# TensorE transposes of the unit matrix ahead of the first norm's, and VectorE's small edge operations moved behind the first weight split

## The chip, the cores and the metric

One Trainium2 chip, one core of it. The metric is the device time of one execution in microseconds (us); the kernel before took 716.55 us (median of 3 runs, 715.22 to 717.28).

## What is computed

A graph layer on 384 nodes of width 1024, in float32. The input is normalised, goes through two attention branches side by side, and then through a routed feed-forward attention:

```python
xn = _layernorm(x, axis=-1)
x = x + gnn(xn, edge_index, edge_type, ...) + mix(xn, ...)      # both: 16 heads of 64, 384 x 384 scores
x = x + ffn(_layernorm(x, axis=-1), ...)                        # three hard-routed trees, then attention
```

Only the beginning concerns this change. `mix` makes q, k, v by `x @ Wqkv`; from k it also makes a row of weights, `softmax(sigmoid(relu(k @ W1 + b1) @ W2 + b2))`. `gnn` adds a mask to its scores, which is built from the edge list: `mask[src, dst] = softplus(w)[type - 1]`, the last edge of a pair counting. For the mask the kernel needs softplus of four weights, and for each edge the key `src * 384 + dst`, compared with the keys of the others, so that an earlier duplicate is dropped.

## The kernel before, in words

The weights come as a stream of units, each 1024 x 256 (1 MB), numbered in the order of use: unit 0 (`U_K0`) is the first K of `mix`, unit 1 (`U_A0`) the first of the other branch's projections, unit 2 (`U_Q0`) the first Q. SyncE loads a unit into one of two `raw` slots (L437 for units 0 and 1, L462 for the rest; unit n is loaded once the low part of unit n - 2 has been made). Every product is done in three passes with rounded operands: each float32 value is split into a high part (`w_hi`, `act_hi`) and the rest (`w_lo`, `act_lo`), and hi x hi, lo x hi and hi x lo are added up in PSUM. The high part of a unit is made by ScalarE (`split_hi`, L777; for unit 0 by GpSimd, L503), the low part by VectorE (`split_lo`, L1264) or, for ten units, unit 1 among them, by GpSimd (L476).

The order on each engine is written out by hand, and semaphores tie the engines together. At the start:

- VectorE takes the statistics of the three tiles of 128 rows (`norm`, L1325), and ScalarE scales each tile into `nat` (L841).
- TensorE waits for `consts_ready` (the unit matrix `ident`, made by GpSimd, L480), and `norm_T` (L1952) transposes tile t in eight pieces of 128 x 128, four to a bank, as soon as `nat` of tile t is there. ScalarE copies each bank into `act_hi` (`take_norm`, L829), VectorE subtracts to get `act_lo` (`take_norm`, L1346).
- Between the `take_norm`s of tiles 0, 1 and 2 VectorE has five small operations (L1461 to L1465): half a bias, |w| of the four edge weights (L1462, its two tensor inputs are the same four columns of `pp`, in SBUF), the edge columns cast to float, and the keys (L1465, two SBUF inputs too). ScalarE's Exp at L925 waits for L1462 by `soft_v`; GpSimd reads the results behind its split of unit 1.
- After them comes `split_lo` of unit 0 (L1468), then the copy of the triangle into PSUM (L1471), and then `key_tile(0)` to `key_tile(12)`, 51 comparisons of the edges' keys in all (L1415), put between VectorE's other work. The keys of all edges, in a row, arrive by `key_a` and `key_b` (L442, L443).
- TensorE's first product, unit 0, runs its first half pass by pass (`hi_first`: L1904, L1907, L1912), since `w_lo` comes last; `gemm_T` (L1888) does the rest with three matmuls to a step (L1921). Unit 1 begins when the first bank of unit 0 has been taken by ScalarE (`take_K`, L799) and VectorE (L1300), and within unit 1 stand two products of the hidden layer (L2017), the second of which waits for ScalarE's eviction of the first (L885), which stands on ScalarE behind `split_hi` of unit 2.

Of the kernel before, what the change touches and what calls it, by code (L numbers as in the profile page):

```python
# [28 lines left out]
P = 128  # L29
N = 384  # L30
D = 1024
NT = N // P
# [29 lines left out]
U_K0, U_A0, U_Q0 = 0, 1, 2  # L62
# [15 lines left out]
def w_slot(n):  # L78

    return n % 4 if n >= U_SORT else n % 2  # L80


def raw_slot(n):

    return n % 2 if n < U_DEEP else (n - U_DEEP) % 4
# [164 lines left out]
def program(nc, x, wstream, ecols, erows, pp_in, table, w1m, w2m, bo, bout, nodes, leaf_b, krow, xs, xsel, hs, ys, yv, out):  # L250
    with ExitStack() as ctx:
        def sb(name, shape, dt):
            return ctx.enter_context(nc.sbuf_tensor(name, shape, dt))
# [10 lines left out]
        def sem(name):  # L264
# [3 lines left out]
        ident = sb("ident", [P, P], F32)  # L268
# [5 lines left out]
        slots01, pad, tile8 = 2 * KT * MB, 1024, KT * N  # L274
        to_x, to_q, to_k, to_v = (slots01 + pad + i * tile8 for i in range(4))
        (w4_hi,), (_, act_hi), (_, w1_raw, w1_hi, w1_lo, row_e), (_, mask01), (_, mask0, diag, erow_i, erow), (_, key_a), \
            (_, oTm_hi, oTg_hi, y_acc, node_raw, node_hi, node_lo, neg_leaf, nsel, h_tmp, dec, lev1, lev2, lev3, sel,
             counts, before, rowf, starts, groupf, ones_b, tri_b), \
            (_, hq_win), (_, raw2, xg2), (vf_hi, _, pTf_hi, _, kf_hi, qf_hi, hT_hi, hT_lo), (_, pf_ring) = region(
                "region_hi", 68,  # L280
                [("w4_hi", [P, 4 * KT, MB], F32R)],
# [74 lines left out]
        def bank(name):  # L356
            return ctx.enter_context(nc.psum_tensor(name, [P, 512], F32))
# [4 lines left out]
        o_bank = bank("o_bank")  # L362
# [60 lines left out]
        def flat(a):  # L423
            return a.rearrange("p a b -> p (a b)")
# [828 lines left out]
        def _(dve):  # L1253
# [7 lines left out]
            def split_lo(n):  # L1261
                to = w_slot(n.base)
                dve.wait_ge(w_hi_ready, n.value(1, 1))
                V.tensor_tensor(flat(w_lo[to][:, :, :]), raws[raw_slot(n.base)], flat(w_hi[to][:, :, :]), ALU.subtract) \  # L1264
                 .then_inc(w_lo_ready, 1)
# [3 lines left out]
            def g_hi_wait(f):  # L1269

                late = f.base >= fill_of(Index(U_OUT)).value()
                dve.wait_ge(g_hi, (f + (-2 * GROUPS if late else 0)).value(1, 1))
# [52 lines left out]
            def norm(src, n, t, chunks):  # L1325

                for c in chunks:
                    last = V.bn_stats(stats[:, t, 6 * c:6 * c + 6], src[:, t, c * 512:(c + 1) * 512])
                own.done(last)
                own.done(V.bn_aggr(mv[:, t, :], stats[:, t, 0:12]))  # L1330
                col = slice(t, t + 1)
                own.done(V.tensor_scalar(ve[:, col], mv[:, t, 1:2], EPS, None, ALU.add))
                V.reciprocal(nmr[:, col], ve[:, col]).then_inc(ln_v, 1)
                dve.wait_ge(ln_root, NT * n + t + 1)

                own.done(V.scalar_tensor_tensor(ntmp[:, col], rstd[:, col], ve[:, col], rstd[:, col], ALU.mult, ALU.mult))
                own.done(V.tensor_scalar(ntmp[:, col], ntmp[:, col], -0.5, 1.5, ALU.mult, ALU.add))
                own.done(V.tensor_tensor(rstd[:, col], rstd[:, col], ntmp[:, col], ALU.mult))
                V.scalar_tensor_tensor(nmr[:, col], mv[:, t, 0:1], -1.0, rstd[:, col], ALU.mult, ALU.mult) \
                 .then_inc(ln_v, 1)  # L1340

            def take_norm(fill0, t):
                for j in range(2):
                    g_hi_wait(Index(fill0 + 2 * t + j))
                    at = act_lo[:, 4 * j:4 * j + 4, t * P:(t + 1) * P]
                    V.tensor_tensor(at, ln_bank[fill0 > 0][t][j][:, :].rearrange("p (k n) -> p k n", n=P),  # L1346
                                    act_hi[:, 4 * j:4 * j + 4, t * P:(t + 1) * P], ALU.subtract).then_inc(g_free, 1)
# [108 lines left out]
            for t in range(NT):  # L1456
                dve.wait_ge(x_in[t], 16)
                norm(x_sb, 0, t, (0, 1))
            take_norm(0, 0)
            dve.wait_ge(small_in, 32)  # L1460
            V.tensor_scalar(halfb2[0:HG, :], pp[0:HG, C_MB2:C_MB2 + 1], 0.5, None, ALU.mult).then_inc(half_ready, 1)  # L1461
            V.scalar_tensor_tensor(wtmp, etw, -1.0, etw, ALU.mult, ALU.max).then_inc(soft_v, 1)  # L1462
            own.done(V.tensor_copy(flat(ecol[:, :, :]), flat(ecol_i[:, :, :])))
            take_norm(0, 1)
            V.scalar_tensor_tensor(ekey[:, :], ecol[:, 0, :], float(N), ecol[:, 1, :], ALU.mult, ALU.add) \  # L1465
             .then_inc(key_ready, 1)
            take_norm(0, 2)
            split_lo(Index(U_K0))  # L1468
            dve.wait_ge(consts_ready, 3)
            dve.wait_ge(key_ready, 1)  # L1470
            own.done(V.tensor_copy(tri_bank, tri[:, :]))  # L1471
# [396 lines left out]
        def _(pe):  # L1868
# [83 lines left out]
            def norm_T(n, fill0, t):  # L1952

                pe.wait_ge(ln_a, NT * n + t + 1)
                for j in range(2):
                    if t == 0:
                        pe.wait_ge(g_free, fill0 + j + 1)
                    for k in range(4 * j, 4 * j + 4):
                        last = nc.tensor.transpose(ln_bank[n][t][j][:, k % 4 * P:(k % 4 + 1) * P],
                                                   nat[:, t, k * P:(k + 1) * P], ident[:, :])  # L1960
                    last.then_inc(g_full, 1)
# [67 lines left out]
            def weights_T(g):  # L2029
# [5 lines left out]
                              start=True, stop=True)  # L2035
                last.then_inc(t_full, 1)

            pe.wait_ge(consts_ready, 1)
            for t in range(NT):
                norm_T(0, 0, t)  # L2040
            first = Index(0)

# [347 lines left out]
            for u in range(1, GROUPS):  # L2390
# [25 lines left out]
            _, group = nc.values_load_multi_w_load_instructions(  # L2416
                group_of[0:1, 0:3 * PAIRS], engines=(mybir.EngineType.PE,), min_val=0, max_val=GROUPS - 1,
                skip_runtime_bounds_check_because="a count of three comparisons")
# [282 lines left out]
```

## Time and profile before

| | |
|---|---|
| median of 3 runs | 716.55 us (715.22 to 717.28) |
| the profiled execution, its own time | 718.01 us |
| its span, first to last instruction | 716.2 us |
| mean granted TensorE clock | 0.998 |
| TensorE matmuls | 688.7 us busy, 4371 instructions |
| VectorE, ScalarE, GpSimd | 479.3, 403.8, 247.9 us busy |
| HBM | 99.35 MB read, 22.49 MB written |

Times are us from the span's start. PE is TensorE (PEld its weight loads), DVE VectorE, ACT ScalarE, POOL GpSimd, SP SyncE. `<-` names what an operation reads, and in square brackets stands the idle time of the engine just before it, with what ended it. Where several instructions of one line follow each other they stand in one row, with their count.

### The profile page before, as it was taken

The page shows a single profiled execution, that of the slowest core. Times are in us where ns is not written, and L with a number is a line of the kernel's source. Part 1 is how long each engine was busy: PE and PEld are TensorE (multiplying, and loading weights), DVE is VectorE, ACT ScalarE, POOL GpSimd, SP SyncE. Part 2 cuts the span into 40 slices and gives each one's busy share as a digit, 9 for nine tenths or more (in the row PEclk, how much of TensorE's full clock was granted, in tenths as well). Part 3 has the DMA queues.
Part 4 walks back from the last instruction along what each step waited for, and adds up shares of the span by engine and source line. Part 5 has one row for each costly group of instructions (what it writes and reads, how often), then busy time and mean ns, then how long its engine had stood idle before and what let it go on. Part 6 is the DMA issues. An engine that isn't in the chain of part 4 may idle for free.

```text
span 716.2 us, 11638 instructions
## 1 busy us (share of the span) xinstructions
PE 688.7 (96%) x4371; PEld 649.2 (91%) x4371; DVE 479.3 (67%) x965; ACT 403.8 (56%) x702; POOL 247.9 (35%) x232
## 2 busy tenths in 40 slices
PE   3999999999999999999999999999999799989997
PEld 3989999998999999999999999998899788779795
DVE  6778756784687487775666665657764667785634
ACT  5655645665556465668586875422522566675541
POOL 5744112132332242228031283472017821341240
PEclk9999999999999999999999999999999999999999
DMA  7822463431332313321313152233169879996242
GB/s 249 320 108 109 186 234 127 169 118 64 121 120 102 117 60 118 109 102 60 118 60 118 60 210 77 108 122 132 46 239 327 280 247 371 347 378 255 114 152 88
DMA packets 25095, 115.38 MB, mean 161 GB/s; under 512 B 7248, under 2 KB 7680, under 8 KB 15968
## 3 DMA queue, kind: packets, MB, share of 16 engines
q1 hardware_dynamic: 14144, 85.05, 32.6%
q0 software_dynamic: 10464, 29.39, 11.4%
q8 instruction: 36, 0.59, 0.3%
q10 hardware_dynamic: 432, 0.20, 0.1%
q14 instruction: 19, 0.16, 0.1%
HBM read 99.35 MB, written 22.49 MB: 170 GB/s over the span
## 4 chain that ended last, share of the span: by engine, by line
PE 79%; DVE 9%; ACT 4%; DMA 4%; issue 3%; POOL 1%; POOLq 0%; ACTq 0%; DVEq 0%
PE g_bank L1921 34%; PE g_bank L1946 12%; PE o_bank L1998 5%; PE t_bank L1987 4%; DVE w_lo L1264 3%; PE s_bank L2278 2%; PE s_bank L1975 2%; PE s_bank L1976 2%; ACT w_hi L777 2%; PE t_bank L2278 2%; PE g_bank L1875 1%; DMA b_raw<-leaf_b_dram 1%; PE s_bank L2508 1%; PE s_bank L2506 1%; PE s_bank L2507 1%
## 5 line engine op out<-in xcount | busy, mean ns | idle before, releaser
L1921 PE MATMUL g_bank<-act_hi,w_hi 128*128 128x384 f32 x488 | 169.3, 347 | 0.2 <-DVE v_st L1291 0.2
L1921 PE MATMUL g_bank<-act_hi,w_lo 128*128 128x384 f32 x488 | 163.6, 335 | 0.0
L1921 PE MATMUL g_bank<-act_lo,w_hi 128*128 128x384 f32 x488 | 163.3, 335 | 0.0
L777 ACT ACTIVATE w_hi<-raw 128x2048 fp32r<-128x2048 f32 x67 | 128.2, 1913 | 48.8 <-PE s_bank L2278 12.5
L1264 DVE TENSOR_TENSOR w_lo<-raw,w_hi 128x2048 fp32r<-128x2048 f32 x58 | 135.7, 2340 | 29.4 <-ACT w_hi L777 28.6
L533 POOL DMA_INDIRECT edge_table<-ew,eidx x51 | 62.0, 1216 | 173.9 <-DMA edge_table<-ew,eidx 170.8
L1921 PEld LDWEIGHTS g_bank<-act_hi,w_hi 128*128 128x128 f32 x488 | 91.8, 188 | 3.1 <-issue 3.0
L1921 PEld LDWEIGHTS g_bank<-act_lo,w_hi 128*128 128x128 f32 x488 | 91.9, 188 | 0.0
L1921 PEld LDWEIGHTS g_bank<-act_hi,w_lo 128*128 128x128 f32 x488 | 91.6, 188 | 0.0
L476 POOL TENSOR_TENSOR w_lo<-raw,w_hi 128x2048 fp32r<-128x2048 f32 x10 | 46.9, 4692 | 99.0 <-ACT w_hi L777 95.0
L1401 DVE TENSOR_TENSOR pT_lo<-t_bank,pT_hi 128x384 fp32r<-128x384 f32 x96 | 50.6, 554 | 33.7 <-ACT pT_hi L870 33.2
L870 ACT ACTIVATE pT_hi<-t_bank 128x384 fp32r<-128x384 f32 x96 | 43.7, 490 | 43.8 <-PE t_bank L1987 43.0
L1946 PE MATMUL g_bank<-w_hi,act_hi 128*128 128x256 f32 x192 | 55.6, 290 | 0.0
L1946 PE MATMUL g_bank<-w_hi,act_lo 128*128 128x256 f32 x192 | 54.3, 283 | 0.0
L1946 PE MATMUL g_bank<-w_lo,act_hi 128*128 128x256 f32 x192 | 54.3, 283 | 0.0
L860 ACT ACTIVATE p_ring<-s_bank,small 128x384 f32<-128x384 f32 x48 | 31.9, 670 | 22.5 <-DVE small L1370 22.5
L1987 PE MATMUL t_bank<-ident,p_ring 128*128 128x128 f32 x288 | 42.2, 273 | 1.8 <-DVE pT_lo L1401 1.1
L1987 PEld LDWEIGHTS t_bank<-ident,p_ring 128*128 128x128 f32 x288 | 34.2, 140 | 5.6 <-issue 4.2
L1946 PEld LDWEIGHTS g_bank<-w_lo,act_hi 128*128 128x128 f32 x192 | 36.7, 191 | 0.0
L1946 PEld LDWEIGHTS g_bank<-w_hi,act_hi 128*128 128x128 f32 x192 | 36.7, 191 | 0.0
L1946 PEld LDWEIGHTS g_bank<-w_hi,act_lo 128*128 128x128 f32 x192 | 36.7, 191 | 0.0
L1975 PE MATMUL s_bank<-k_st,q_st 128*128 128x384 f32 x96 | 32.3, 337 | 0.6 <-DVE junk L1415 0.6
(329 smaller groups left out, 1617.9 us busy)
## 6 DMA issues: line engine op xcount, KB each, us to landing
raw<-wstream_dram SPq DMA_DIRECT2D x68, 1024.0 KB, 8.0
xg<-xs POOLq DMA_DIRECT2D x12, 512.0 KB, 4.7
ys<-y_ring POOLq DMA_DIRECT2D x12, 512.0 KB, 7.7
yv<-y_ring POOLq DMA_DIRECT2D x12, 256.0 KB, 2.3
key_b<-edge_keys SPq DMA_DIRECT2D x1, 1728.0 KB, 10.7
x_sb<-x_dram SPq DMA_DIRECT2D x3, 512.0 KB, 4.8
key_a<-edge_keys SPq DMA_DIRECT2D x1, 1536.0 KB, 6.9
y_acc<-x_dram POOLq DMA_DIRECT2D x3, 512.0 KB, 5.3
```

Source lines behind the costliest of these rows:

```text
L476: nc.gpsimd.tensor_tensor(flat(w_lo[to][:, :, :]), raws[raw_slot(n)], flat(w_hi[to][:, :, :]), ALU.subtract).then_inc(w_lo_pool, 1)
L533: nc.gpsimd.indirect_dma_start(table, bass.IndirectOffsetOnAxis(ap=eidx[:, e:e + 1], axis=0), ew[:, e:e + 1], None, bounds_check=N * N - 1 ...
L777: nc.scalar.activation(flat(w_hi[to][:, :, :]), raws[s], ACT.Copy).then_inc(w_hi_ready, 1)
L860: ins = nc.scalar.activation(tile, s_bank[q.slot(3)][:, 0:N], ACT.Exp, bias=nbias[:, s:s + 1], scale=alpha[:, c:c + 1], accum_out=esum[:, ...
L870: nc.scalar.activation(pT_hi[:, :, t * P:(t + 1) * P], t_bank[f.slot(2)][:, 0:N].rearrange("p (m n) -> p m n", n=P), ACT.Copy).then_inc(t_ ...
L1264: V.tensor_tensor(flat(w_lo[to][:, :, :]), raws[raw_slot(n.base)], flat(w_hi[to][:, :, :]), ALU.subtract) \
L1401: V.tensor_tensor(pT_lo[:, :, cols], t_bank[f.slot(2)][:, 0:N].rearrange("p (m n) -> p m n", n=P), pT_hi[:, :, cols], ALU.subtract).then_i ...
L1921: last = mm(out, w2[a], x2[b], start=k == 0 and a + b == 0, stop=not after and k == KT - 1 and a == 1)
L1946: last = mm(out, x2[a], w2[b], start=k == 0 and a + b == 0, stop=k == KT - 1 and a == 1)
L1975: mm(out, q_st[:, m, a, c], k_st[:, m, a, :], start=True, stop=False)
L1987: last = nc.tensor.transpose(t_bank[f.slot(2)][:, m * P:(m + 1) * P], p_ring[:, q.slot(PR), m * P:(m + 1) * P], ident[:, :])
L1998: last = mm(o_bank[:, 0:N], v_st[:, m, h, :, :].rearrange("p a d -> p (a d)"), p[:, m, :], start=c == 0, stop=c == len(todo) - 1)
```

## The change

Two edits. VectorE takes all three norm tiles first, then makes the low part of unit 0, and only then does the five small operations. TensorE, before it waits for the norm of tile 0, 1 and 2, transposes the unit matrix 44, 14 and 18 times into `o_bank`, a bank that nothing uses until the hidden layer.

```diff
@@ -1456,16 +1456,15 @@
             for t in range(NT):
                 dve.wait_ge(x_in[t], 16)
                 norm(x_sb, 0, t, (0, 1))
-            take_norm(0, 0)
+            for t in range(NT):
+                take_norm(0, t)
+            split_lo(Index(U_K0))
             dve.wait_ge(small_in, 32)
             V.tensor_scalar(halfb2[0:HG, :], pp[0:HG, C_MB2:C_MB2 + 1], 0.5, None, ALU.mult).then_inc(half_ready, 1)
             V.scalar_tensor_tensor(wtmp, etw, -1.0, etw, ALU.mult, ALU.max).then_inc(soft_v, 1)
             own.done(V.tensor_copy(flat(ecol[:, :, :]), flat(ecol_i[:, :, :])))
-            take_norm(0, 1)
             V.scalar_tensor_tensor(ekey[:, :], ecol[:, 0, :], float(N), ecol[:, 1, :], ALU.mult, ALU.add) \
              .then_inc(key_ready, 1)
-            take_norm(0, 2)
-            split_lo(Index(U_K0))
             dve.wait_ge(consts_ready, 3)
             dve.wait_ge(key_ready, 1)
             own.done(V.tensor_copy(tri_bank, tri[:, :]))
@@ -2035,8 +2034,14 @@
+            def keep_busy(count):
+
+                for _ in range(count):
+                    nc.tensor.transpose(o_bank[:, 0:P], ident[:, :], ident[:, :])
+
             pe.wait_ge(consts_ready, 1)
             for t in range(NT):
+                keep_busy((44, 14, 18)[t])
                 norm_T(0, 0, t)
             first = Index(0)
```

## Rows read from the trace of the kernel before

**Rows 1.** The page: busy time by engine, and the chain by engine.

```profile
PE 688.7 (96%) x4371; PEld 649.2 (91%) x4371; DVE 479.3 (67%) x965; ACT 403.8 (56%) x702; POOL 247.9 (35%) x232
...
PE 79%; DVE 9%; ACT 4%; DMA 4%; issue 3%; POOL 1%; POOLq 0%; ACTq 0%; DVEq 0%
```

**Rows 2.** The chain that ended last, 15 to 30 us: start, us, what.

```profile
15.01 1.97 PE t_bank L1959 x8
16.98 2.83 PE g_bank L1904 x8
19.81 1.64 PE g_bank L1907 x8
21.45 1.39 PE g_bank L1912 x8
22.83 6.76 PE g_bank L1921 x39
```

**Rows 3.** Windows: stretch, us, busy of five engines (instructions), PEclk, DMA share, GB/s.

```profile
17.00:20.00 3.00, 3.00 (x10) 3.00 (x11) 3.00 (x5) 2.96 (x4) 0.25 (x1) 1.00 0.98 336
```

**Rows 4.** Windows of PE alone: stretch, us, busy (matmuls), PEclk, DMA, GB/s.

```profile
570.00:571.00 1.00, 1.00 (x7) 0.50 0.96 397
...
573.00:574.00 1.00, 1.00 (x10) 0.91 0.99 418
```

**Rows 5.** Timeline of PE, two sets behind long pauses: start, us, what.

```profile
569.72 1.91 PE L2361 MATMUL t_bank<-ident,xg 128*128 128x128 f32 x8 [2.56 <-DVE xT_lo L1746]
...
628.02 1.09 PE L2361 MATMUL t_bank<-ident,xg 128*128 128x128 f32 x8 [1.90 <-DMA xg<-ys,row_of]
```

**Rows 6.** Two sets of eight transposes: one's ns min/median/max, first and last start in us.

```profile
L1959 PE MATMUL g_bank<-ident,nat x8: 421/421/447, 9.0 to 10.5; 128*128 128x128 f32 x8
...
L2361 PE MATMUL t_bank<-ident,xg x8: 270/272/273, 553.0 to 553.7; 128*128 128x128 f32 x8
```

**Rows 7.** Timeline of VectorE, ScalarE and TensorE, 16 to 50 us.

```profile
16.17 0.60 ACT L829 ACTIVATE act_hi<-t_bank 128x512 fp32r<-128x512 f32 x1 [0.72 <-PE t_bank L1959]
...
17.24 1.28 DVE L1346 TENSOR_TENSOR act_lo<-t_bank,act_hi 128x512 fp32r<-128x512 f32 x2
...
17.77 1.90 ACT L777 ACTIVATE w_hi<-raw 128x2048 fp32r<-128x2048 f32 x1
18.44 2.28 DVE L1264 TENSOR_TENSOR w_lo<-raw,w_hi 128x2048 fp32r<-128x2048 f32 x1
...
22.30 0.35 DVE L1415 SCALAR_TENSOR_TENSOR junk<-key_a,ekey,s_bank 128x128 bf16<-128x128 f32 x1 [1.38 <-DMA key_a<-edge_keys]
...
23.89 1.12 DVE L1300 TENSOR_TENSOR k_st<-g_bank,k_st 64x384 fp32r<-64x384 f32 x2 [0.43 <-ACT k_st L799]
...
28.05 1.12 DVE L1300 TENSOR_TENSOR k_st<-g_bank,k_st 64x384 fp32r<-64x384 f32 x2 [0.91 <-ACT k_st L799]
...
29.56 1.92 ACT L777 ACTIVATE w_hi<-raw 128x2048 fp32r<-128x2048 f32 x1 [1.54 <-issue]
31.50 0.59 ACT L885 ACTIVATE hid<-o_bank,pp 128x384 f32<-128x384 f32 x1
...
32.73 0.33 PE L2017 MATMUL o_bank<-k_st,w_hi 128*128 128x384 f32 x1
...
49.68 1.13 DVE L1312 TENSOR_TENSOR q_lo<-g_bank,q_st 64x384 fp32r<-64x384 f32 x2 [1.58 <-ACT q_st L812]
```

**Rows 8.** Timeline: GpSimd's long operations, and VectorE's short ones beside them.

```profile
13.82 1.89 POOL L503 CAST w_hi<-raw 128x2048 fp32r<-128x2048 f32 x1 [4.25 <-DVE small L1339]
...
14.86 0.87 DVE L1462 SCALAR_TENSOR_TENSOR small<-pp 128x4 f32<-128x4 f32 x1
...
19.75 5.43 POOL L476 TENSOR_TENSOR w_lo<-raw,w_hi 128x2048 fp32r<-128x2048 f32 x1 [4.04 <-ACT w_hi L777]
...
51.53 4.59 POOL L476 TENSOR_TENSOR w_lo<-raw,w_hi 128x2048 fp32r<-128x2048 f32 x1 [4.88 <-ACT w_hi L777]
...
54.63 1.50 DVE L1370 TENSOR_TENSOR small<-small 128x1 f32<-128x1 f32 x1
```

## The prediction

> **What bounds the kernel.** I read the page first: TensorE is busy for 96% of the span, and 79% of the chain of waits is its own work [rows 1]. So a us taken from TensorE's chain is a us of the end, if nothing else takes its place. Next the chain at the start, since both edits lie before 23 us. From 15.01 us on it is TensorE alone: the transposes of the last tile, then the three passes of unit 0's first half [rows 2]. The passes are alike, eight matmuls of 384 columns, but take 2.83, 1.64 and 1.39 us: 0.354, 0.205 and 0.174 us a matmul. The clock column says 1.00 there, with 10 matmuls in 3 us [rows 3]. A stretch where the column does say 0.50 shows what the slow level (1.2 GHz against 2.4) looks like: seven matmuls in a us, and ten once it reads 0.91 [rows 4]; eight transposes took 1.91 us in it, against 1.09 at 628 us [rows 5]. The eight at 9.0 us took 0.42 us each, those at 553 us 0.27 [rows 6]. So TensorE runs at the slow level until about 20.3 us, inside the second pass, whatever the column says. It had then worked without a pause since 15.01, 5.3 us, and with pauses since 9.00. What the slow level costs the chain is 2.83 - 1.39 + 1.64 - 1.39 = 1.7 us, plus part of the transposes.
>
> **Part 1, the added transposes.** There are 76. They overlap, so one costs the step from start to start: 1.5 / 7 = 0.214 us slow and 0.7 / 7 = 0.10 us fast [rows 6]. I take 0.217 and 0.108, the higher by the rounding of those starts. They start when the unit matrix is ready, at about 1.6 us, and the first 44 are covered by TensorE's idle 9.00 us. If the clock rises after 3.4 us of unbroken work (what the stretch of [rows 4] saw, from the first transposes at 569.8 to the rise inside 573 to 574) or after 5.3 (the start), they end at 8.0 or 9.1 us: no delay either way, since ScalarE only reads the first transposed tile at 11.8, after scaling the second. Then 14 x 0.108 = 1.5 us in a pause of 0.9 to 2.0, and 18 x 0.108 = 1.9 us in the next: TensorE finishes a tile about 1.0 us after its norm in place of 1.9, so the pauses are about 2 us and hold them. Cost nothing; the cover is the wait for the norm, and where it is gone is rival 3. I take it that dense transposes raise the clock: the slow stretch in which it rose again at 573 us began with eight of them, unbroken with the matmuls behind [rows 4, 5].
>
> What it brings: the last tile's transposes start at 15.01 as before (the norm sets that), but its first bank, four transposes, is full after about 0.6 us in place of 1.1. ScalarE copies it from 15.6 instead of 16.17 [rows 7] and the second to 16.75 instead of 17.62. The high pass, whose second half needs that copy (4 x 0.174 us), then ends at 17.6 instead of 19.81.
>
> **Part 2, the move on VectorE.** The low parts of the norm now follow one another and end about 0.1 us behind 0.6 us of work on the bank copied at 16.75: at 17.45 instead of 17.24 + 1.28 = 18.52 [rows 7]. The low pass runs 17.6 to 19.0. The split of unit 0 takes 2.28 us and ends at 19.74 instead of 20.72; TensorE waits for it from 19.0, does the last pass until 21.15 instead of 22.83, and the second half of unit 0 (24 x 0.173 = 4.16 us) until 25.3 instead of 27.0. So far 1.7 us ahead.
>
> Now the five small operations. In the old place L1462, four elements, took 0.87 us, and it ended at 15.73, with GpSimd's cast (13.82 + 1.89 = 15.71). The same again at 54.63: one element from two SBUF inputs took 1.50 us and ended at 56.13, GpSimd's split at 56.12. And GpSimd's split of unit 1 took 5.43 us where the same at 51.53 took 4.59: it began at 19.75 while VectorE's split of unit 0 ran until 20.72 [rows 7, 8]. So on this core a VectorE operation with two SBUF inputs and a GpSimd operation on SBUF don't run side by side: the later waits for the whole of the earlier. The Trainium skill says what these rows show (GPSIMD Engine Reference, "1. Specifications": GpSimd's SBUF interfaces are shared with VectorE, and contend with VectorE instructions with two SBUF inputs); by it the sum has the stall that follows, without it rival 1's time.
>
> In the new place, ScalarE ends the high part of unit 1 at about 19.1 (0.65 us earlier than 19.67), GpSimd is issued at 19.2, waits for VectorE's split until 19.74 and then holds for 4.59 us, to 24.35. L1462 comes at 19.9, has two SBUF inputs, and stands until 24.35: a stall of 4.4 us. Queued behind it on VectorE: the cast, the keys and the triangle's copy (0.2 us each, as the copy, which ended at 22.30 - 1.38 = 20.92), so `key_tile(0)` starts at 25.0 instead of 22.30, ends after 1.16 us (22.30 to 23.89 - 0.43), and the low part of K's first bank, 1.12 us, is done at 27.4 instead of 25.01 [rows 7]. ScalarE's Exp of L925 waits for the same stall, with K's eviction behind it; at most 2 x 0.59 us later, at 25.8, that is done, before VectorE comes. Unit 1 needs this bank free: TensorE, ready at 25.3, starts at 27.4 instead of 27.0. **Sum: 1.7 us gained by 25.3, 2.1 us of waiting, 0.4 us lost.**
>
> Next down the path: the second hidden product, at 32.73 before, comes at 33.15. ScalarE's high part of unit 2 (29.56 before, when its load lands) can start at about 29.9, once K's second bank is taken, so the hidden layer's eviction ends near 32.4: in time. K's second bank is free by 31.1, and is wanted at 32.2. GpSimd's mask work starts 2.4 us later (it waits for VectorE's softplus) and has 4.1 us of slack before its next split. SyncE's and GpSimd's queues are otherwise unmoved: the key loads depend on neither edit, unit 2's load is issued 1.0 us earlier behind them. From there the chain alternates between engines that wait for each other (VectorE still has 1.58 us idle before the last low part of Q, at 49.68 [rows 7]), so I let the 0.4 us pass to the end: 718.01 + 0.4 = 718.4 for an execution like the profiled one, which stood 1.46 above the median; for the median, 716.55 + 0.4 = 717.0.
>
> **The rivals.**
> 1. *No stall at L1462*, four elements slipping in ahead of GpSimd, or another rule for the port. Then K's low part is free by 24.6, and unit 1 starts at 25.3. But ScalarE's high part of unit 2 began at 29.56 after 1.54 us idle, waiting for the load, which queues behind the keys with the DMA engines at a share of 0.98 [rows 3, 7]; the hidden eviction still ends at 32.1, and the second hidden product can't start before: 0.6 us gained of the 1.7, 716.0. If the load lands sooner as well, up to 1.7: 714.85. Against it: three rows at two places. Chance 0.22.
> 2. *The new pause costs the clock.* TensorE stands from 25.3 to 27.4, 2.1 us. A pause of 2.56 us was followed by the slow level, one of 1.90 not (its transposes took 1.09) [rows 5]. If the clock falls, 3.4 us at half speed cost 1.7 more: +2.1, 718.7. It decides from a pause somewhere between those two. Chance 0.14.
> 3. *The transposes don't raise the clock*, the case that ends clearly slower. For it: the sets of eight at 9.0 and at 15.01 us, the last unbroken with what follows, were both slow [rows 2, 6]. Then 44 x 0.217 = 9.5 us end at 11.1; with the sets of eight (1.74 each), 3.0 and 3.9 us, the last tile is done at 23.3 instead of 16.98, 6.3 us late, and with the stall on VectorE some 7: 723.6. Chance 0.07. The Trainium skill speaks for this one (TensorE: Matmul & The Clock Gate, "Part 4: PE-mode transpose": a transpose does not count as work for the clock gate as a matmul does); the mixed stretch at 570 us neither refutes nor bears it out.
>
> **How the numbers follow.** Forecast (stall, clock kept) 0.50, rivals 0.22, 0.14, 0.07, and 0.07 for what I don't see, of either sign. A measurement here can't tell 0.3%, 2.15 us, from no change. The forecast and rival 1 lie within it (up to -1.7), rival 2 on its edge (half counted as slower), rival 3 beyond. Faster 0.07, same 0.78, slower 0.15. The range goes from rival 1's far end to rival 2: 714.8 to 718.8; it leaves out rival 3 and the unseen.
>
> **What would show it.** Right: L1904, L1907 and L1912 at about 1.4 us each; a wait of TensorE for `w_lo` before L1912; L1462 at some 4.4 us, ending with GpSimd's L476; TensorE idle for about 2 us before unit 1, released by VectorE's L1300. Wrong: L1462 under 0.5 us, or K's first bank taken before 25.3; transposes still at 1.9 us a set of eight at 15 us; or unit 1's matmuls 0.35 us apart after the pause.

## The result, and the profile after

| | before | after |
|---|---|---|
| median of 10 runs, us | 716.59 (715.22 to 717.62) | 718.58 (716.66 to 721.01) |
| ratio of the runs | | 1.0026, 95% interval 1.0015 to 1.0037 |
| profiled execution, us | 718.01 | 716.66 |
| its span, us | 716.2 | 714.9 |

The predicted 717.0 is 1.6 us short of the median, and the median lies inside the range (714.8 to 718.8), near its upper end. It is 0.28% above before: slower, but by less than the 0.3% that the forecast called no change. Against before the loss is 2.0 us, where the forecast had 0.4. Measured again later, the same kernel gave 718.49 us (12 runs) against 717.24 (34 runs): 1.0016 (1.0001 to 1.0031). Of all the runs in this text one, of 726.75 us, was in the chip's rarer slow state, and no ratio uses it.

One trap first. The profiled execution of after is the fastest of its ten, and that of before is slower than all ten beside it. Subtracting one from the other says that the change gains 1.35 us, and the twenty runs say that it loses. So the two traces are compared below by stretch, never by their ends.

The page: busy time by engine, and the chain by engine.

```profile
PE 694.1 (97%) x4447; PEld 654.1 (92%) x4447; DVE 482.8 (68%) x965; ACT 403.7 (56%) x702; POOL 254.6 (36%) x232
...
PE 79%; DVE 10%; ACT 4%; DMA 3%; issue 2%; POOL 1%; POOLq 0%; ACTq 0%; DVEq 0%
```

TensorE has its 76 more instructions. The shares of the chain move by 1%, which would be 7 us, and the effect is 2: these two lines don't say where it is. TensorE's timeline over the start:

```profile
1.60 6.94 PE L2040 MATMUL o_bank<-ident 128*128 128x128 f32 x44 [1.60 <-POOL ident L480]
9.13 1.09 PE L1958 MATMUL g_bank<-ident,nat 128*128 128x128 f32 x8 [0.58 <-ACT nat L841]
...
12.95 2.13 PE L2040 MATMUL o_bank<-ident 128*128 128x128 f32 x18
15.19 1.09 PE L1958 MATMUL t_bank<-ident,nat 128*128 128x128 f32 x8
16.62 1.65 PE L1903 MATMUL g_bank<-act_hi,w_hi 128*128 128x384 f32 x8 [0.34 <-ACT act_hi L829]
18.11 1.55 PE L1906 MATMUL g_bank<-act_lo,w_hi 128*128 128x384 f32 x8
20.05 1.66 PE L1911 MATMUL g_bank<-act_hi,w_lo 128*128 128x384 f32 x8 [0.39 <-DVE w_lo L1264]
27.80 0.41 PE L1920 MATMUL g_bank<-act_hi,w_hi 128*128 128x384 f32 x1 [1.92 <-DVE k_st L1300]
```

A set of eight takes 1.09 us where the last took 1.97 [rows 2], and the first pass 1.65. The same view of before, the first pass and the start of unit 1:

```profile
16.91 2.90 PE L1904 MATMUL g_bank<-act_hi,w_hi 128*128 128x384 f32 x8
...
26.83 0.33 PE L1921 MATMUL g_bank<-act_hi,w_hi 128*128 128x384 f32 x1
```

The rise shows directly in the windows (stretch, us, busy with the matmuls, PEclk, DMA share, GB/s): eleven transposes in 2 us, then nine in 1 us. The record of the clock puts the rise at 5.57 us, after 4 us of nothing but transposes (4.38 to 7.52 us in the traces of the other kernels that have them); the PEclk column says 1.00 on both sides of it.

```profile
3.00:5.00 2.00, 2.00 (x11) 1.00 0.99 370
5.00:6.00 1.00, 1.00 (x9) 1.00 1.06 381
```

The last row of after's timeline is the price: TensorE stands 1.92 us ahead of unit 1 and starts it at 27.80, where it started without a pause at 26.83. VectorE and GpSimd say why:

```profile
19.10 5.37 POOL L476 TENSOR_TENSOR w_lo<-raw,w_hi 128x2048 fp32r<-128x2048 f32 x1 [3.22 <-ACT w_hi L777]
...
19.92 0.13 DVE L1463 TENSOR_SCALAR small<-pp 4x1 f32<-4x1 f32 x1
19.98 4.51 DVE L1464 SCALAR_TENSOR_TENSOR small<-pp 128x4 f32<-128x4 f32 x1
24.42 0.23 DVE L1465 CAST ecol<-ecol_i 128x153 f32<-128x153 int32 x1
24.68 0.21 DVE L1466 SCALAR_TENSOR_TENSOR ekey<-ecol 128x51 f32<-128x51 f32 x1
25.00 0.29 DVE L1470 COPY s_bank<-tri 128x128 f32<-128x128 f32 x1
26.53 1.12 DVE L1300 TENSOR_TENSOR k_st<-g_bank,k_st 64x384 fp32r<-64x384 f32 x2
```

Four elements to a partition take 4.51 us and end with GpSimd's split. The chain that ended last goes through that one operation (start, us, what):

```profile
15.19 0.67 PE t_bank L1958 x4
...
15.88 0.61 ACT act_hi L829
...
16.51 1.29 DVE act_lo L1346 x2
17.80 2.20 DVE w_lo L1264
...
20.05 4.45 DVE small L1464
...
25.33 1.16 DVE junk L1415 x8
...
27.09 0.57 DVE k_st L1300
27.66 0.14 issue
27.80 2.35 PE g_bank L1920 x12
```

Unit 1 comes 0.97 us later than before, and the matmuls from the second hidden product on 1.07 to 1.11 later, up to 560 us. Of that, 0.18 is the load of the input, which landed at 4.82 us against 4.64 here: the start costs 0.8 at unit 1 and 0.9 from the second hidden product on. Then two things near 560 us turn the order of the two executions round. At 561.02 us before's TensorE waits 1.50 us, as in no other of the fourteen traces (0.02 to 0.07 there); whether that is luck or before's way, one trace of before can't say. And, luck as other traces show, the pause of 2.56 us before the transposes at 569.78 was not followed by the slow level in after, so the stretch of [rows 4, 5] is missing, and with it 1.5 us. The first row is of before, the second of after:

```profile
561.02 0.88 PE L2448 MATMUL s_bank<-ident,hc 128*128 128x128 f32 x6 [1.50 <-DVE hc L1696]
...
569.78 1.16 PE L2366 MATMUL t_bank<-ident,xg 128*128 128x128 f32 x8 [2.56 <-DVE xT_lo L1745]
```

### The profile page after: what moved, and what is told of

Same layout as the page of the kernel before. It is cut to its first block, busy times and chain, and to the rows that moved or that the text cites. A ratio compares the mean times of both kernels' runs of the same rounds, so it can differ in the third digit from the quotient of the medians.

```text
span 714.9 us, 11789 instructions
## 1 busy us (share of the span) xinstructions
PE 694.1 (97%) x4447; PEld 654.1 (92%) x4447; DVE 482.8 (68%) x965; ACT 403.7 (56%) x702; POOL 254.6 (36%) x232
## 4 chain that ended last, share of the span: by engine, by line
PE 79%; DVE 10%; ACT 4%; DMA 3%; issue 2%; POOL 1%; POOLq 0%; ACTq 0%; DVEq 0%
PE g_bank L1920 34%; PE g_bank L1945 12%; PE o_bank L1997 5%; PE t_bank L1986 4%; DVE w_lo L1264 3%; PE s_bank L2283 2%; DMA ys<-y_ring 2%; PE s_bank L1974 2%; PE s_bank L1975 2%; PE t_bank L2283 2%; PE g_bank L1874 1%; PE s_bank L2513 1%; PE s_bank L2511 1%; PE s_bank L2512 1%; ACT w_hi L777 1%
## 5 line engine op out<-in xcount | busy, mean ns | idle before, releaser
L1264 DVE TENSOR_TENSOR w_lo<-raw,w_hi 128x2048 fp32r<-128x2048 f32 x58 | 135.9, 2343 | 28.8 <-ACT w_hi L777 27.4
L533 POOL DMA_INDIRECT edge_table<-ew,eidx x51 | 69.5, 1363 | 165.4 <-DMA edge_table<-ew,eidx 159.2
```

The lines of the kernel that those rows point to most:

```text
L533: nc.gpsimd.indirect_dma_start(table, bass.IndirectOffsetOnAxis(ap=eidx[:, e:e + 1], axis=0), ew[:, e:e + 1], None, bounds_check=N * N - 1 ...
```

## The experiments

All twelve are shown against before, whose runs are shared within a group. The groups were run apart, the third on another chip than the first two (median of before 717.16, 717.24, 716.33), so ratios are compared across groups and times are not. The second measurement of after belongs to the second group. It was expected at 1.7 to 2.0 us over before, with most mean clocks at 0.993 to 0.995, or, if the clock had no share, at 1.0 us over with clocks like before's. It came 1.25 us over, with 5 of 12 runs at 0.995 or less against 20 of 34 of before: nearer the second. "Unit 1" is the start of its first matmul in the profiled execution, 26.83 in before; the "second hidden product" starts at 32.73 there. Before has one trace, and its input landed at 4.64 us, the earliest of all (4.77 to 5.36 elsewhere); a lead or a lag is given as it stands in the trace, and the later input is named where it matters.

### First group: the two halves apart, the stall, the pause

**VectorE's move alone** (no added transposes).

```diff
-                keep_busy((44, 14, 18)[t])
```

> The move on VectorE alone, none of the added transposes. Theory (the two-input operation stands until GpSimd's split of unit 1 ends): L1462 takes about 4.4 us and ends with GpSimd's L476 near 25.2 us; unit 1 starts at about 28.5 us instead of 26.8, TensorE idle 1.7 us before it; 716.6 + 1.7 = 718.3 us, up to 719 if the pause costs clock in some runs. Rival (the added transposes are what costs, the move is free or gains): 716.6 us or less.

Measured: 719.38 us, 1.0034 (1.0018 to 1.005). L1464 stalls as in after, and unit 1 comes at 29.05, 2.2 late, of which 0.7 is a later input in that execution and 1.5 the move's. The pause is 1.30 us, and was expected at 1.7:

```profile
21.24 4.51 DVE L1464 SCALAR_TENSOR_TENSOR small<-pp 128x4 f32<-128x4 f32 x1
29.05 0.41 PE L1920 MATMUL g_bank<-act_hi,w_hi 128*128 128x384 f32 x1 [1.30 <-DVE k_st L1300]
```

The move by itself loses, with no transposes that could be blamed.

**The transposes alone** (VectorE in the order of before).

> The added transposes alone, VectorE's order as before. Theory: no stall behind the split, unit 0's three passes at full clock, but the low part of unit 0 still comes at about 21.0 us behind the small operations, so TensorE waits for it and unit 1 starts at about 26.4 us instead of 26.8: 716.2 us, not slower than before. Rival (the transposes themselves cost, by clock or by delay): 718 us or more.

Measured: 716.12, 0.9986 (0.9973 to 1.0). The passes run fast, but the second and the third wait for VectorE: the last starts at 21.09, only 0.2 earlier than before, and unit 1 at 26.75, not at the 26.4 that was expected.

```profile
16.77 1.63 PE L1904 MATMUL g_bank<-act_hi,w_hi 128*128 128x384 f32 x8 [0.34 <-ACT act_hi L829]
18.90 1.69 PE L1907 MATMUL g_bank<-act_lo,w_hi 128*128 128x384 f32 x8 [0.50 <-DVE act_lo L1346]
21.09 1.66 PE L1912 MATMUL g_bank<-act_hi,w_lo 128*128 128x384 f32 x8 [0.51 <-DVE w_lo L1264]
```

Neither half pays at the start: one brings a clock that VectorE can't feed, the other frees VectorE and puts its small operations behind a stall. The median of the transposes alone is 1.0 us under before all the same, with an interval that reaches 1.0; the start, 0.1 us ahead with the input 0.25 later, explains 0.3 of that.

**The small operations between the last norm and the split.**

```diff
             for t in range(NT):
                 take_norm(0, t)
-            split_lo(Index(U_K0))
             dve.wait_ge(small_in, 32)
...
              .then_inc(key_ready, 1)
+            split_lo(Index(U_K0))
             dve.wait_ge(consts_ready, 3)
```

> As the kernel after, but the small operations stand between the last norm tile's low part and the split of unit 0, where GpSimd is idle. Theory: L1462 takes 0.2 us, the split ends near 20.8 us, no pause before unit 1, which starts at about 26.3 us; then 0.5 us ahead of before: 716.1 us, 2.5 less than after. Rival (another of the change's effects makes the loss): stays near 718.6 us.

Measured: 716.02, 0.9987 (0.9973 to 1.0001); on another chip 715.26, 0.9987 (0.9974 to 0.9999). No stall, since GpSimd is idle at that time, and no pause before unit 1 (26.23); the four (the text ahead says five, but lists four) cost 0.5 us together, which puts the split and the last pass back by as much:

```profile
17.76 0.14 DVE L1463 SCALAR_TENSOR_TENSOR small<-pp 128x4 f32<-128x4 f32 x1
18.21 2.29 DVE L1264 TENSOR_TENSOR w_lo<-raw,w_hi 128x2048 fp32r<-128x2048 f32 x1
...
19.09 5.88 POOL L476 TENSOR_TENSOR w_lo<-raw,w_hi 128x2048 fp32r<-128x2048 f32 x1 [3.22 <-ACT w_hi L777]
...
20.55 1.68 PE L1911 MATMUL g_bank<-act_hi,w_lo 128*128 128x384 f32 x8 [0.91 <-DVE w_lo L1264]
```

So the operation itself is worth 0.14 us, and 4.37 of its 4.51 are the neighbour. But 0.7 us ahead at the last pass has shrunk to 0.2 at the second hidden product (32.56). That is taken up in the third group. The second measurement was made for the median: with so little lead left it was expected within 0.5 us of before's, or, if the 1.1 us of the first were real and came from elsewhere, 1 us under it again. It was 1.07 under: the second of the two, and from where stays open (end of the third group).

**The pause filled**: 18 more transposes of the unit matrix between units 0 and 1.

```diff
             gemm_T(Index(U_K0), act_hi, act_lo, T_X, hi_first=True)
+            keep_busy(18)
             gemm_T(Index(U_A0), act_hi, act_lo, T_X, between=in_A)
```

> The kernel after with 18 more transposes of the unit matrix behind unit 0, in the pause of 2.1 us before unit 1. The stall stays: unit 1 at 27.8 us as after. Theory (about half of the loss is the clock, which falls in the pause in most runs): 716.6 + 1.0 = 717.6 us with a mean granted clock of 0.998 in most runs, 1.0 less than after. Rival (the slow stretches lie elsewhere, or cost nothing): 718.6 us, clock 0.993 to 0.995 as after.

Measured: 717.87, 1.0003 (0.9994 to 1.0012), with unit 1 at 27.92. Run again beside after it gave 717.90, 1.0003 (0.9992 to 1.0015), and after there 718.49, 1.0016 (1.0001 to 1.0031); expected were 0.7 to 1.0 us over before and 1 less than after. Both times the filled pause is the quicker, by some 0.6 us where they ran together, but the two intervals overlap, and there the mean clocks were alike (0.9966 and 0.9968): a hint that the pause costs something beyond its length, not a proof, and no sign that it is the clock.

### Second group: is it the two inputs in SBUF?

**One input by way of PSUM.** The order of after; the two operations with two SBUF inputs get one of them through a copy in a score bank that is idle then.

```diff
+            dve.wait_ge(g_free, 2 + 2 * NT)
...
-            V.scalar_tensor_tensor(wtmp, etw, -1.0, etw, ALU.mult, ALU.max).then_inc(soft_v, 1)
+            own.done(V.tensor_copy(s_bank[2][:, 128:132], etw))
+            V.scalar_tensor_tensor(wtmp, s_bank[2][:, 128:132], -1.0, etw, ALU.mult, ALU.max).then_inc(soft_v, 1)
...
-            V.scalar_tensor_tensor(ekey[:, :], ecol[:, 0, :], float(N), ecol[:, 1, :], ALU.mult, ALU.add) \
+            own.done(V.tensor_copy(s_bank[2][:, 256:256 + ET], ecol[:, 1, :]))
+            V.scalar_tensor_tensor(ekey[:, :], ecol[:, 0, :], float(N), s_bank[2][:, 256:256 + ET], ALU.mult, ALU.add) \
```

> The order of after, but the two small operations with two SBUF inputs (L1464 and the keys at L1466) get one input from PSUM, where a copy of four columns and one of 51 put it. Theory (two SBUF inputs are what waits): no stall, L1464 takes some 0.2 us beside GpSimd's split, the first comparison of keys starts when the keys land, near 22.5 us, unit 1 starts at about 25.7 us instead of 27.8, no pause; then the second hidden product waits for ScalarE until 32.2: 0.5 us ahead of before, some 2.5 less than after. Rival (any short operation of VectorE stands behind a long one of GpSimd): the first of these operations takes 4.4 us as in after, and the time stays.

Measured: 718.28, 1.0009 (0.9996 to 1.0023). A miss that taught most:

```profile
19.06 5.36 POOL L476 TENSOR_TENSOR w_lo<-raw,w_hi 128x2048 fp32r<-128x2048 f32 x1 [3.21 <-ACT w_hi L777]
...
20.11 0.16 DVE L1466 SCALAR_TENSOR_TENSOR small<-s_bank,pp 128x4 f32<-128x4 f32 x1
20.19 4.32 DVE L1467 CAST ecol<-ecol_i 128x153 f32<-128x153 int32 x1
27.91 0.57 PE L1923 MATMUL g_bank<-act_hi,w_hi 128*128 128x384 f32 x1 [2.05 <-DVE k_st L1300]
```

The added wait in front costs nothing here: the first small operation starts right behind the split, at 19.88. The operation of the prediction now takes 0.16 us beside GpSimd, and the cast behind it, with a single input, stalls for 4.32 us in its place. And the pause, 2.05 us, was followed by the slow level (windows of TensorE: stretch, us, busy with the matmuls, PEclk, DMA share, GB/s):

```profile
28.00:29.00 1.00, 1.00 (x4) 0.50 0.97 410
29.00:30.00 1.00, 1.00 (x5) 0.50 1.00 410
...
31.00:32.00 1.00, 1.00 (x7) 0.79 0.06 25
32.00:33.00 1.00, 1.00 (x7) 1.00 0.00 0
```

The matmuls 1.07 us behind before at the start of unit 1 are 2.71 behind once the clock is back: 1.6 us more. This is rival 2, seen as it happens in one execution; the median is 1.0 us over before's, and what the clock did there in the other runs is not known.

**The same, and the hidden layer's first eviction ahead of ScalarE's split of unit 2.**

```diff
-            split_hi(Index(U_Q0))
             hidden(Index(0), 0)
+            split_hi(Index(U_Q0))
```

> As the kernel before this one, and ScalarE takes the first hidden product ahead of the high part of unit 2, whose load lands at 29.5 us. Theory (that order capped the gain): the second hidden product runs near 31.5 us instead of 32.2 or later, 1.2 us ahead of before in all: 715.5 us where before is 716.6. Rival (the load of unit 2 or VectorE's low part of it ends last anyway): the same as the kernel before this one.

Measured: 718.95, 1.0021 (1.0007 to 1.0034). The pause was 2.07 us and the clock fell again (1.7 us more), so in the profiled execution the eviction came late and put the split back from 30.30 to 33.78. While unit 1 is late the swap gains nothing.

### Third group: no stall at all, then what hides the gain

**All small operations past GpSimd.** Each of them behind the split reads or writes PSUM; the full cast goes behind `key_tile(1)`.

```diff
+            dve.wait_ge(g_free, 2 + 2 * NT)
...
-            V.scalar_tensor_tensor(wtmp, etw, -1.0, etw, ALU.mult, ALU.max).then_inc(soft_v, 1)
-            own.done(V.tensor_copy(flat(ecol[:, :, :]), flat(ecol_i[:, :, :])))
-            V.scalar_tensor_tensor(ekey[:, :], ecol[:, 0, :], float(N), ecol[:, 1, :], ALU.mult, ALU.add) \
-             .then_inc(key_ready, 1)
+            own.done(V.tensor_copy(s_bank[2][:, 128:132], etw))
+            V.scalar_tensor_tensor(wtmp, s_bank[2][:, 128:132], -1.0, etw, ALU.mult, ALU.max).then_inc(soft_v, 1)
+            own.done(V.tensor_copy(s_bank[2][:, 256:256 + 2 * ET], ecol_i[:, 0:2, :].rearrange("p a b -> p (a b)")))
+            own.done(V.tensor_copy(ecol[:, 1, :], s_bank[2][:, 256 + ET:256 + 2 * ET]))
+            V.scalar_tensor_tensor(ekey[:, :], s_bank[2][:, 256:256 + ET], float(N), ecol[:, 1, :],
+                                   ALU.mult, ALU.add).then_inc(key_ready, 1)
...
             key_tile(1)
+            own.done(V.tensor_copy(flat(ecol[:, :, :]), flat(ecol_i[:, :, :])))
```

> The order of after, with every small operation behind the split having PSUM as its source or its destination: |w| from a copy of four columns in PSUM, the key columns cast into PSUM and added from there, and the full cast of the edge columns put behind the second comparison tile, when GpSimd's split is over. Theory (two SBUF inputs, or a copy from SBUF to SBUF, stand behind GpSimd; PSUM on either side does not): none of them over 0.4 us, the first key comparison starts when the keys land, near 22.7 us, unit 1 at about 25.7 us with no pause, the second hidden product at 32.2 to 32.6 us behind ScalarE's high part of unit 2; 0.2 to 0.5 us ahead of before. Rival: another operation takes the stall (4.3 us) and unit 1 stays at 27.8.

Measured: 715.21, 0.9979 (0.9968 to 0.999).

```profile
19.34 5.36 POOL L476 TENSOR_TENSOR w_lo<-raw,w_hi 128x2048 fp32r<-128x2048 f32 x1 [3.22 <-ACT w_hi L777]
20.39 0.16 DVE L1466 SCALAR_TENSOR_TENSOR small<-s_bank,pp 128x4 f32<-128x4 f32 x1
20.47 0.26 DVE L1467 CAST s_bank<-ecol_i 128x102 f32<-128x102 int32 x1
...
29.94 1.92 ACT L777 ACTIVATE w_hi<-raw 128x2048 fp32r<-128x2048 f32 x1 [2.53 <-issue]
31.88 0.58 ACT L885 ACTIVATE hid<-o_bank,pp 128x384 f32<-128x384 f32 x1
32.61 0.41 PE L2020 MATMUL o_bank<-k_st,w_hi 128*128 128x384 f32 x1 [0.60 <-ACT hid L885]
```

The cast of the two columns that the keys need, written to PSUM, takes 0.26 us beside GpSimd; nothing stalls, and unit 1 starts without a pause, 0.9 us ahead of before although the input landed 0.4 later. Then the gain goes: ScalarE stands 2.53 us for the load of unit 2 (issued at 20.3 us, landed after 9.6), splits it, and only then evicts the hidden product for which TensorE waits 0.60. The second hidden product comes at 32.61, 0.12 ahead, and from 34 us on the matmuls are level with before's.

**The same, and the hidden eviction ahead of that split** (the swap of the last run of the second group).

> As e7, and ScalarE takes the first hidden product ahead of the high part of unit 2. Theory (that order is what caps the gain): the second hidden product at about 31.5 us instead of 32.73, 1.2 us ahead of before, 0.8 less than e7. Rival (TensorE is then held by something else within 12 us of it): the same as e7.

Measured: 714.51, 0.9979 (0.9965 to 0.9994).

```profile
29.41 0.58 ACT L885 ACTIVATE hid<-o_bank,pp 128x384 f32<-128x384 f32 x1 [2.04 <-PE o_bank L2020]
29.91 1.92 ACT L777 ACTIVATE w_hi<-raw 128x2048 fp32r<-128x2048 f32 x1
31.75 0.33 PE L2020 MATMUL o_bank<-k_st,w_hi 128*128 128x384 f32 x1
```

The split starts when it did, since it waits for the load; the eviction fits ahead of it, and the product comes 1.0 us ahead, without a wait. That lead was still 0.8 from 217 us on. Between the two, the runs don't tell which is quicker: their intervals are nearly the same. Both beat before, by 0.06 to 0.35% in their intervals, and their intervals lie below after's.

**The order of the third experiment with the same swap.**

> The small operations ahead of the split (as e3), and ScalarE takes the first hidden product ahead of the high part of unit 2. Theory: unit 1 at 26.1 us as in e3, the second hidden product at about 31.9 us instead of e3's 32.56: 0.9 us ahead of before, 0.7 less than e3. Rival: the same as e3.

Measured: 715.50, 0.9983 (0.9972 to 0.9995), second hidden product at 32.28; without the swap it stood at 32.47 on the same chip. Between the two orders nothing is left that the runs can tell.

**What the start doesn't explain.** The transposes alone, the order of the third experiment and the first kernel of this group are 0.9 to 1.5 us quicker than before by their ratios, and their starts explain 0.2 to 0.5 of that: at 34 us they stand 0.15 us ahead of before or less, with inputs that landed 0.15 to 0.4 us later. The cause of the rest is not shown. The mean clocks of their runs are 0.9976 to 0.9986, of before's 0.9968 in both groups; a slow stretch of 3.4 us takes 0.0024 off that mean and costs 1.5 to 1.7 us, so by my estimate the clock is worth 0.5 to 1.2 us of it. Where in the kernel it is kept, and why, is open. The other candidate is before's wait of 1.50 us at 561 us, which no trace of another kernel has; only more traces of before could tell how often it comes.

## Why the prediction was right, and where its sum was off

**The transposes raise the clock: right.** Added transposes alone did it, in every trace that has them. Rival 3 is out. Against it stand eleven transposes in 2 us, then nine in 1 us, with no other work on TensorE. The Trainium skill (TensorE: Matmul & The Clock Gate, "Part 4: PE-mode transpose") says that full speed does not engage for transposes, since they don't count as busy the same way; for the float32 transposes of this kernel the measurement decides, and says otherwise. The sets of eight at 9.0 and 15.01 us that I listed for it [rows 2, 6] had pauses ahead of them; with the pauses filled the same sets take 1.09 us.

**The stall at L1462: right, with its length.** Forecast some 4.4 us, measured 4.51 (the line is L1464 in after), and 0.14 with GpSimd idle. It is in all five traces that have this operation behind the split with both inputs in SBUF, and in no other trace does the operation take longer than before's 0.87. Rival 1 fell: nothing slips in ahead. The reason that the prediction gave, two inputs in SBUF, was too narrow. A cast with one input, SBUF to SBUF, stood 4.32 us; with PSUM on one side the |w| operation took 0.16 and a cast of two of the three columns 0.26. Queued behind L1464 the cast cost nothing more, so the sum was not hurt; the experiment that rested on the narrow reading was.

**Unit 1's start: right in kind, mis-sized by 0.6 us.** The sum gave 27.4 against 27.0, 0.4 lost; the trace has 27.80 against 26.83, 0.97 lost. The 0.57 between them splits so:
- 0.17: before's unit 1 starts at 26.83, not the 27.0 that I worked out;
- 0.26: "the cast, the keys and the triangle's copy (0.2 us each)". From the cast's start to `key_tile(0)` I had 0.65 us; these operations wait for one another, and start 0.26, 0.32 and 0.33 us apart, 0.91 in all;
- 0.07: the cast behind the stall starts at 24.42, not 24.35, with the input 0.18 us later in this execution, which is no part of the change;
- 0.07: from `key_tile(0)` to unit 1 it was 2.47 us (25.33 to 27.80), not 2.40, in gaps between the engines.

On the way "1.7 us gained by 25.3" was too much, and bore no weight, since the pause swallows it either way: the matmuls of unit 0's second half come 1.1 us ahead of before, and the pause is 1.92 us. The first pass ended at 18.1, not 17.6, since it starts when the first bank has been copied and then runs eight matmuls without a gap, and it took 0.19 us a matmul, not 0.174. The split of unit 0 ended at 20.00 (19.74), and the stall's end is set by GpSimd all the same.

**Downstream: right.** ScalarE's split of unit 2 starts at 30.20, the hidden eviction at 32.14, the second hidden product comes at 33.80: 1.07 behind before, and none of it is made up before 560 us.

**From the start to the median: open.** The sum passed 0.4 on to the end, and the medians are 2.0 apart. The trace would pass on 0.9, its 1.07 less the late input, 0.12%. The first measurement says 1.5 to 3.7 thousandths, the second 0.1 to 3.1. The second agrees with the start alone; the first wants at least 0.2 us more. So the forecast had the way and the mechanism, and less than half of the start's loss. That the median still lies in the range is in part luck: the range reached up to 718.8 for rival 2, and that rival 2 brought it there isn't shown. For it: of the profiled executions with a pause ahead of unit 1, those of 1.30, 1.91 and 1.92 us kept the clock, and those of 2.05 and 2.07 lost it, at 1.6 to 1.7 us each, and after's is 0.13 us short of the shorter of these. But the length alone does not decide: at 628 us seven of the fourteen traces have pauses of 2.00 to 2.31 us, and all kept the clock. The spread of after's ten runs, 4.4 us against 2.4, says little either: in the second measurement it is 5.6 against 4.7. Against a large share: with the pause filled, the kernel was quicker by only 0.6 us, within the intervals; and the mean clock of after's runs was 0.9959 and 0.9968, of before's 0.9963 to 0.9968 in the three groups, hardly apart. How many of its executions lose the clock there, only traces of many of them could say.

**What rival 1 was right about.** Its condition was false, but its cap was real: once the stall was gone, 0.9 us gained by unit 1 and 0.12 left after ScalarE's split of unit 2. It named the load as the gate; the gain could be had in the trace all the same by taking the eviction out from behind the split (-1.0 us at the second hidden product). I took an order in ScalarE's queue for a limit of the memory. The median did not keep to the cap: it fell by 1.1 us, where rival 1 had 0.6 (see what the start doesn't explain).

## What to carry to other kernels

Before moving a small VectorE operation behind a large one, look what GpSimd does at the new time: four elements to a partition cost 0.14 us beside an idle GpSimd and 4.51 beside a long one, and the price falls on everything queued behind. If it must sit there, let one side of it be PSUM, which passed here in every case. Where an earlier start fades, look for the engine that stands waiting for one thing while holding another that is ready: here one swapped pair of calls kept 0.97 us of lead at the second hidden product, where 0.12 had been left, though the medians don't tell the two kernels apart.

## What the runs showed that was not expected

- A one-input VectorE cast of 128x153 elements from SBUF to SBUF stood 4.32 us beside GpSimd's split and took 0.23 without it. Copies and casts with PSUM on one side (0.14, 0.21, 0.26, 0.29 us) and a 4x1 scalar operation (0.13 us) passed. The Trainium skill (GPSIMD Engine Reference, "1. Specifications") names instructions in a 2-port mode beside those with two SBUF inputs; whether the cast ran in one, no trace here says. In both cases the wait lasted until GpSimd's whole instruction was done.
- It works the other way too. GpSimd's split takes 5.37 us when it starts 0.9 us before VectorE's split ends, and 5.88 when it starts 1.4 before (third experiment), against 4.59 alone [rows 8].
- The same pause can go either way. The 2.56 us ahead of the last-stage transposes were followed by the slow level in before and in the first kernel of the third group (eight transposes in 1.91 and 1.94 us), and not in after (1.16 us); of the fourteen traces nine lost the clock there.
- The PEclk column reads 1.00 ahead of the first change of clock in a trace, where the instructions run at half speed (a transpose every 0.21 us, then every 0.108). There their spacing has to be read in its place.
